# FFN transposes moved from TensorE to VectorE squares and a trip through DRAM, `down` two blocks behind, weights issued by GpSimd

## The reference, cut to what matters

```python
logits = jnp.einsum('btd,de->bte', x, gate_w)
probs = jax.nn.softmax(logits, axis=-1)
expert_weights, expert_indices = jax.lax.top_k(probs, TOP_K)
...
for i in range(E):
    wi = jnp.where(expert_indices == i, expert_weights, 0.0).sum(-1)
    h = jax.nn.silu(jnp.einsum('btd,df->btf', x, w1[i])) * jnp.einsum('btd,df->btf', x, w3[i])
    out = out + jnp.einsum('btf,fd->btd', h, w2[i]) * wi[..., None]
```

## Time and profile before

| | |
|---|---|
| median of 3 runs | 488.11 us (488.01 to 489.12) |
| the profiled execution: its own time | 488.38 us |
| its span, first to last instruction | 486.7 us |
| TensorE matmuls busy | 422.2 us (87% of the span) |
| VectorE busy | 257.6 us (53%) |
| ScalarE busy | 192.5 us (40%) |
| GpSimd busy | 157.4 us (32%) |
| moved by DMA | 50.92 MB |
| mean granted clock of TensorE | 0.935 of full |

### The profile page before, as it was taken

How to read it: one execution, slowest core, us unless ns; L and a number is a source line. 1 busy time by engine, 2 the same in 40 slices (tenths; PEclk the granted TensorE clock), 3 DMA queues, 4 the chain that set the end, 5 groups by cost and what they waited for, 6 DMA issues and landing times.

```text
span 486.7 us, 10406 instructions
## 1 busy us (share of the span) xinstructions
PE 422.2 (87%) x2557; PEld 367.1 (75%) x2558; DVE 257.6 (53%) x673; ACT 192.5 (40%) x334; POOL 157.4 (32%) x130
## 2 busy tenths in 40 slices
PE   0668985237999999999999999999999999999980
PEld 0556874225788888888889888888888898888870
DVE  7877867988454356433553653365355334652230
ACT  3446445113343354334544453444455224542220
POOL 5454440022033224222532342243235222432321
PEclk9979795558899999999999999999999999999996
DMA  6856788300718111911137118112811211111120
GB/s 196 303 179 211 262 267 248 132 23 22 272 24 282 31 32 22 291 32 22 22 71 252 22 27 285 32 22 46 277 22 22 32 32 22 24 30 32 22 32 11
DMA packets 33076, 50.92 MB, mean 105 GB/s; under 512 B 3335, under 2 KB 25095, under 8 KB 33063
## 3 DMA queue, kind: packets, MB, share of 16 engines
q1 hardware_dynamic: 24983, 38.44, 23.7%
q0 software_dynamic: 8080, 12.33, 13.0%
HBM read 39.36 MB, written 11.40 MB: 104 GB/s over the span
## 4 chain that ended last, share of the span: by engine, by line
PE 75%; DVE 5%; issue 2%; DMA 2%; POOL 1%; ACT 0%; DVEq 0%; POOLq 0%; ACTq 0%
PE bank L1319 65%; PE bank L1342 6%; PE bank L1326 2%; PE bank L1252 1%; DMA dg<-depool_rows,plugi 1%; DMA out<-yblk,itok 1%; PE bank L1273 1%; POOL dg L441 1%; DVE split L1117 0%; DVE split L321 0%; DVE batch L985 0%; PE bank L1198 0%; POOL out L480 0%; DVE onehot_lo L981 0%; DVE st L818 0%
## 5 line engine op out<-in xcount | busy, mean ns | idle before, releaser
L1319 PE MATMUL bank<-split,xT_hi 128*128 x592 | 167.9, 406 | 5.4 <-DVEq L1136 4.1
L1091 DVE TENSOR_TENSOR hmul<-gact,bank 128x512 f32<-128x512 f32 x74 | 50.9, 688 | 148.5 <-ACT gact L609 148.5
L1319 PEld LDWEIGHTS bank<-split,xT_hi 128*128 128x128 f32 x592 | 107.7, 192 | 27.0 <-issue 6.1
L480 POOL DMA_INDIRECT out<-yblk,itok x37 | 79.2, 2140 | 150.9 <-ACT yblk L616 143.4
L1319 PE MATMUL bank<-split,hT 128*128 (+1 forms) x888 | 115.2, 286 | 1.0 <-DVE hT L1097 0.7
L1319 PEld LDWEIGHTS bank<-split,hT 128*128 128x128 f32 x888 | 108.5, 191 | 1.4 <-DVE hT L1097 0.9
L609 ACT ACTIVATE gact<-bank 128x512 f32<-128x512 f32 x74 | 44.2, 598 | 164.3 <-PE bank L1319 153.4
L1319 PE MATMUL bank<-split,xT_lo 128*128 x296 | 94.2, 399 | 0.0
L472 POOL DMA_INDIRECT xblk<-z_rows,gidx x40 | 40.7, 1018 | 108.4 <-DVE gidx L1104 102.5
L321 DVE TENSOR_TENSOR split<-raw,split (+1 forms) x22 | 50.4, 2292 | 37.1 <-ACT split L315 35.9
L1319 PEld LDWEIGHTS bank<-split,xT_lo 128*128 128x128 f32 x296 | 56.2, 190 | 13.6
(11 more groups left out here) (182 smaller groups left out, 309.8 us busy)
## 6 DMA issues: line engine op xcount, KB each, us to landing
raw<-in_L_ffn_w SPq DMA_DIRECT2D x24, 1024.0 KB
ctx_sb<-in_ctx SPq DMA_DIRECT2D x4, 1024.0 KB, 6.4
x_all<-in_x SPq DMA_DIRECT2D x4, 512.0 KB, 8.3
depool_rows<-gact SPq DMA_DIRECT2D x4, 512.0 KB, 3.0
out<-x_all SPq DMA_DIRECT2D x4, 512.0 KB
z_rows<-z SPq DMA_DIRECT2D x4, 512.0 KB, 3.4
xblk<-z_rows,gidx POOLq DMA_INDIRECT x40
out<-yblk,itok POOLq DMA_INDIRECT x37
```

Source lines behind the costliest of these rows:

```text
L480: pool.indirect_dma_start(out[:, :], bass.IndirectOffsetOnAxis(ap=itok[:, q:q + 1], axis=0), yblk[:, q, :], None, compute_op=ALU.add).then ...
L1091: dve.tensor_tensor(hmul[:, cols], gact[:, cols], p_lin[part][:, :], ALU.mult)\
L1319: mm = pe.matmul(out_, xp, w_, start=start and n == 0, stop=stop and n == 2)
```

## The change

- `hT` leaves TensorE for all blocks but the last. VectorE transposes `hmul` in squares of 32 x 32 into `swap_in` (`turn`, one instruction for each half). SP writes `swap_in` (512 KB) to `swap_dram`, waits until it has landed, and reads it back into `swap_out` in another order (`exchange`), which moves the squares to their places. ScalarE makes `hT_hi` from `swap_out` by one instruction of 128 x 1024, and VectorE `hT_lo`.
- `down`, `y`, `meta` and `add_rows` are two blocks behind, not one. Blocks 0 and 1 stand outside of the loop; TABLE has one more column, `blocks_i` holds the count less two, and `drain` transposes the last block on TensorE and then does two `down`.
- ScalarE's `y` stands ahead of the weight split in a step, not behind it.
- `raw_load` of experts 1 to 7 goes from SP to GpSimd.
- For the first expert `lo_ready` is raised by 2 ahead of its w2 part and by 1 behind it; before, by 3 behind it. The list of weights and that split come behind both halves of `h` in the first step.
- The rows of zeros at the end of `out` are written by three transfers, not two.

```diff
-TABLE = 1 + 2 * STEP_PAIRS + 3
+TABLE = 2 + 2 * STEP_PAIRS + 3
+Q = 32
+NQ = P // Q
...
+        swap_dram = nc.dram_tensor("swap_rows", (2, P, F), f32, kind="Internal").ap()
+        swap_in = sb("swap_in", [P, 2, NQ, KF, Q], f32)
+        swap_out = sb("swap_out", [P, 2, NQ, KF, Q], f32)
...
-            body(0, 0, 0, step_word(eng, 0))
+            for i in range(2):
+                body(i, i, 0, step_word(eng, i))
             with eng.Fori(0, STEP_PAIRS) as pair:
-                word = step_word(eng, pair * 2 + 1)
+                word = step_word(eng, pair * 2 + 2)
                 with eng.If(word & F_RUN):
-                    body(pair * 2 + 1, 1, pair, word)
-                    word = step_word(eng, pair * 2 + 2)
+                    body(pair * 2 + 2, 0, pair + 1, word)
+                    word = step_word(eng, pair * 2 + 3)
                     with eng.If(word & F_RUN):
-                        body(pair * 2 + 2, 0, pair + 1, word)
-
-        def block_count(eng):
+                        body(pair * 2 + 3, 1, pair + 1, word)
...
-                for e, m in parts[max(k - 1, 0):k] if k < B + 1 else parts[k - 1:]:
-                    raw_load(sp, e, e, s["raw_ready"] if e else s["raw_first"], (m,))
-
-
-            sp.wait_ge(s["lo_first"], 3)
-            sp.wait_ge(s["raw_ready"], RAW_SEM)
-            sp.wait_ge(s["xT_done"], 1)
-            raw_load(sp, 2, 0, s["raw_ready"])
+                for e, m in parts[max(k - 1, 0):k]:
+                    raw_load(sp, e, e, s["raw_first"], (m,))
+
+
             sp.wait_ge(s["table_ready"], 1)
 
+            def exchange(i, q, half):
+
+                sp.wait_ge(s["swap_ready"], 2 * (i + 1))
+                if after(i, 2):
+                    settle(sp)
+                    sp.wait_ge(s["hTlo_ready"], i - 1)
+                sp.dma_start(swap_dram[q], swap_in[:, q].rearrange("p b k t -> p (b k t)")).then_inc(parked[q], 16)
+                sp.wait_ge(parked[q], 16 * (half + 1))
+                sp.dma_start(swap_out[:, q].rearrange("p a k t -> p a (k t)"),
+                             swap_dram[q].rearrange("(a j) (b c) -> (j b) a c", a=NQ, b=NQ)).then_inc(swapped[q], 16)
+
             def step(i, q, half, word):
-                with sp.If(word & F_LOAD):
-                    e = expert(word).with_bounds(min_val=0, max_val=E - 4)
-                    sp.wait_ge(s["lo_ready"], e * 3 + 6)
-                    settle(sp)
-                    sp.wait_ge(s["raw_ready"], RAW_SEM * (e + 2))
-                    settle(sp)
-                    raw_load(sp, e + 3, (e + 1) & 1, s["raw_ready"])
-
+                exchange(i, q, half)
+
+            less_two = blocks_less_two(sp)
             over_steps(sp, step)
...
+            raw_load(pool, 1, 1, s["raw_ready"])
...
-            def step(i, q):
+            def step(i, q, half, word):
 
                 pool.wait_ge(s["xT_done"], i + 2)
                 block_rows(i + 3, 1 - q)
-                if not isinstance(i, int):
-                    add_rows(i - 1, 1 - q)
-
-            step(0, 0)
-            with pool.Fori(0, STEP_PAIRS) as pair:
-                with pool.If(step_word(pool, pair * 2 + 1) & F_RUN):
-                    step(pair * 2 + 1, 1)
-                    with pool.If(step_word(pool, pair * 2 + 2) & F_RUN):
-                        step(pair * 2 + 2, 0)
-            at_end(pool, blocks, add_rows)
-            pool.wait_ge(s["added_rows"], OUT_INIT + blocks * 16)
+                if after(i, 2):
+                    add_rows(i - 2, q)
+                if not after(i, 1):
+                    pool.wait_ge(s["lo_first"], 3)
+                    pool.wait_ge(s["raw_ready"], RAW_SEM)
+                    settle(pool)
+                    raw_load(pool, 2, 0, s["raw_ready"])
+                with pool.If(word & F_LOAD):
+                    e = expert(word).with_bounds(min_val=0, max_val=E - 4)
+                    pool.wait_ge(s["lo_ready"], e * 3 + 6)
+                    settle(pool)
+                    pool.wait_ge(s["raw_ready"], RAW_SEM * (e + 2))
+                    settle(pool)
+                    raw_load(pool, e + 3, (e + 1) & 1, s["raw_ready"])
+
+            def drain(i, q):
+                add_rows(i - 1, 1 - q)
+                add_rows(i, q)
+
+            over_steps(pool, step)
+            at_end(pool, less_two, drain)
...
             def hT(i, q, half):
-                act.wait_ge(s[f"th{half}_done"], i + 1)
-                act.activation(hT_hi[:, q, half * KF // 2:(half + 1) * KF // 2], p_hT[half][:, :], ACT.Copy)\
-                   .then_inc(s[f"hT{half}hi_ready"], 1)
+
+                act.wait_ge(swapped[q], 16 * half)
+                act.activation(hT_hi[:, q].rearrange("p k (a t) -> p a k t", a=NQ), swap_out[:, q], ACT.Copy)\
+                   .then_inc(s["hThi_ready"], 1)
+
+            def hT_last(i, q, part):
+
+                act.wait_ge(s[f"th{part}_done"], 1)
+                ks = slice(part * KF // 2, (part + 1) * KF // 2)
+                act.activation(hT_hi[:, q, ks], p_hT[part][:, :], ACT.Copy)\
+                   .then_inc(s["drainhi_ready"], 1)
...
-                later = not isinstance(i, int) or i > 0
                 silu(i, 0)
-                if later:
-                    hT(i - 1, 1 - q, 1)
                 xT(i + 1, 1 - q)
                 silu(i, 1)
-                hT(i, q, 0)
+                if after(i, 1):
+                    hT(i - 1, 1 - q, half + q)
+                if after(i, 2):
+                    y(i - 2, q)
+                if not after(i, 1):
+                    act.wait_ge(s["list_mm"], 2)
 
                 with act.If(word & F_CHUNK):
                     e = expert(word)
...
                     with act.If(word & F_W2):
                         with act.If(word & F_W3):
                             split_hi(act, raw3, 1)
-                        if later:
+                        if after(i, 1):
                             act.wait_ge(s["y_done"], i)
                         split_hi(act, raw3, 2)
-                if later:
-                    y(i - 1, 1 - q)
 
             def drain(i, q):
-                hT(i, q, 1)
+
+                hT_last(i, q, 0)
+                hT_last(i, q, 1)
+                y(i - 1, 1 - q)
                 y(i, q)
...
                 dve.tensor_tensor(hmul[:, cols], gact[:, cols], p_lin[part][:, :], ALU.mult)\
                    .then_inc(s[f"h{part}_done"], 1)
 
-            def hT(i, q, part):
+            def turn(i, q, half, part):
+
+                dve.wait_ge(s[f"h{part}_done"], i + 1)
+                if after(i, 2):
+                    dve.wait_ge(parked[q], 16 * half)
                 ks = slice(part * KF // 2, (part + 1) * KF // 2)
-                dve.wait_ge(s[f"hT{part}hi_ready"], i + 1)
+                dve.transpose(swap_in[:, q, :, ks, :].rearrange("p b k t -> p k b t"),
+                              hmul[:, part * HALF:(part + 1) * HALF].rearrange("p (k t b) -> p k b t", b=NQ, t=Q))\
+                   .then_inc(s["swap_ready"], 1)
+
+            def hT(i, q):
+
+                dve.wait_ge(s["hThi_ready"], i + 1)
+                dve.tensor_tensor(hT_lo[:, q].rearrange("p k (a t) -> p a k t", a=NQ), swap_out[:, q],
+                                  hT_hi[:, q].bitcast(f32).rearrange("p k (a t) -> p a k t", a=NQ), ALU.subtract)\
+                   .then_inc(s["hTlo_ready"], 1)
+
+            def hT_last(i, q, part):
+
+                dve.wait_ge(s["drainhi_ready"], part + 1)
+                ks = slice(part * KF // 2, (part + 1) * KF // 2)
                 dve.tensor_tensor(hT_lo[:, q, ks].rearrange("p k t -> p (k t)"), p_hT[part][:, :],
                                   hT_hi[:, q, ks].bitcast(f32).rearrange("p k t -> p (k t)"), ALU.subtract)\
-                   .then_inc(s[f"hT{part}lo_ready"], 1)
+                   .then_inc(s["drainlo_ready"], 1)
...
-                later = not isinstance(i, int) or i > 0
+                if not after(i, 1):
+                    dve.wait_ge(s["lo_first"], 2)
+                    dve.sem_inc(s["lo_ready"], 2)
                 h(i, 0)
-                if later:
-                    hT(i - 1, 1 - q, 1)
-                    meta(i - 1, 1 - q)
                 xT(i + 1, 1 - q)
+                turn(i, q, half, 0)
                 next_index(i + 3, 1 - q, half + q + 1)
-                if not later:
+                h(i, 1)
+                turn(i, q, half, 1)
+                if not after(i, 1):
                     weights_out()
-                h(i, 1)
-                hT(i, q, 0)
-                if not later:
                     split_lo(dve, 0, 0, 2, "lo_first")
                     dve.wait_ge(s["lo_first"], 3)
-                    dve.sem_inc(s["lo_ready"], 3)
+                    dve.sem_inc(s["lo_ready"], 1)
+                if after(i, 1):
+                    hT(i - 1, 1 - q)
+                if after(i, 2):
+                    meta(i - 2, q)
...
-            def down(i, q, e, slot, by_halves=False):
-
```

(91 more changed lines are left out.)

20 lines of the change are left out of this document (11 added, 9 removed).

## The result

The changed kernel takes 515.07 us (median, 514.46 to 518.34) against 488.11: 1.056 of the time before, 95% interval 1.053 to 1.059. It is 27 us slower, where 33.6 us faster was forecast. The profiled execution spans 516.7 us; it is the longest of the five runs (518.34 us by its own time), so sums read from its trace are some 3 us above what the median holds.

A forecast was written before the change was run, and what follows sets the result against it. TensorE, busy 87% of the span, was taken as the bound. Gains of 40.4 us less 3.0 (tail), 0.6 (TABLE) and 3.0 (load stalls) gave -33.8 against 488.38: forecast 454.5 us, range 449 to 474.

The forecast's parts named there:

- The loop at 8.68 us: TensorE's block step in the loop falls from 9.56 to 8.68 us as transposes leave; 32.1 us gone in all.
- the sum without load stalls: Whole kernel's forecast time with no stalls from weight loads: 451.5 us, used for the low end of the range.
- Block 1: At the start, `up` of block 1 comes 4.3 us sooner; full clock gives 1.8 more, new `xT_lo` wait costs 0.7.
- TABLE: Longer list operations and rows of odd length from 43 columns for 42 cost 0.6 us, bounds 0 and 1.5.
- Squares: VectorE's two transposes per block take 0.69 us each, bounds 0.4 and 1.4.
- y of block i-2 now stands ahead of the split: Split starts 0.6 us into the next step; VectorE's split, `h`, `xT_lo` end by 6.5, wanted at 8.68: hidden.
- VectorE's order: Sign of a wrong forecast: TensorE's idle time in the loop names `xT_lo`.
- The round trip: Swap to DRAM and back takes 7.6 us, 10.8 beside a load, mean 8.3; hidden up to 9.4, so costed at nothing.
- Gathers behind the weights: x's gathers queue behind GpSimd's weight loads: 3.0 us forecast for six loads; as a rival 458 to 476 us, chance 0.12.
- The lock of GpSimd by VectorE: Rival: each of three load issues loses 0.95 us to VectorE, 3.4 us stall per load; 472 us, chance 0.05.
- Slower than before: the same loop past its point: Rival: mean round trip over 11.4 us makes the loop step over 9.70; at 12.5 it is 510 us; chance 0.09.
- The tail: After the last step's `down`, three adds come close together and the last goes at about 9.4 us: 3.0 us lost.

The follow-up runs named there:

- experiment 3: Changed kernel with VectorE's `meta` first in its step and the weight loads of experts 2 to 7 cut to 3 x 128 KB: 452.71 us, ratio 0.927.
- experiment 1: Changed kernel with VectorE's `meta` of block i-2 moved first in its step, not behind `hT`: 483.46 us, ratio 0.989.
- 6: Changed kernel with ScalarE's `y` put back behind the weight split and `meta` left where the change has it: 483.29 us, ratio 0.989.
- experiment 2: Changed kernel with the weight loads of experts 2 to 7 cut to 3 x 128 KB, most weights left out: 478.51 us, ratio 0.980.
- experiment 4: Kernel before the change, with only the weights of experts 1 to 7 issued by GpSimd: 483.81 us, ratio 0.993.
- experiment 7: Changed kernel with `meta` first on VectorE and the weights issued by SP behind the exchange of the step: 499.03 us, ratio 1.023.

## Why the prediction was wrong

- *The loop at 8.68 us:* right. It is the step in 11 of 35 here and in 34 of 35 of experiment 3. That its 452.71 us lie beside the sum without load stalls (451.5) is in part luck: the start lost 3.4 us more than reckoned and the tail 3 (both below), and behind the last add 4.8 us went away (11.6 to 6.8) that the sum does not have.
- *Block 1:* right for its own wait. From the x transposes of step 0 to those of step 1 are 7.8 us, where it was 14.4. Of the 6.6 us gained 0.9 are transposes that the sum counts elsewhere; 5.7 are left against 4.3 + 1.8. The new wait for the next `xT_lo` was mis-sized: for 0.7 the next step lost 3.1 us in the changed kernel (a wait of 2.9) and 4.1 in experiment 3 (a wait of 2.5, and the half of `up` behind it at a granted clock of 0.66).
- *TABLE:* 0.6 us forecast. The first x transposes start 0.1 to 0.8 us later in the kernels with it (106.28 to 106.98 for 106.22); how much of this is its doing is not shown.
- *Squares:* mis-sized, 1.105 us against 0.69, inside of the bounds. It makes the ring 0.8 us longer; without it the ring would be 9.7, still over 8.68.
- *"y of block i-2 now stands ahead of the split, so the split starts 0.6 us into the next step ... They are wanted at 8.68: hidden."* **This is the step that failed.** I let y wait for `down` only. It also waits for `meta`, which the change puts behind `hT_lo` on VectorE; I counted `meta` among "copies 0.5". So I listed each engine's load, 7.2 us of 8.68, and one in-order chain (from the trip's landing), and missed the ring that needs no trip. Opening it gave 31.6 us in experiment 1, and by 6 either of its sides can be opened. The largest wait of TensorE, for `xT_lo`, is the sign that the prediction gave for "VectorE's order".
- *The round trip:* right where nothing runs beside it (6.9 us for 7.6), mis-sized beside a load. I took half of the bandwidth, as one 128 KB gather suggested, and 10.8 us; it was 12.7 (7.56 and 5.10), with up to 11.3 for one read. But the mean was right: 8.45 us over the 37 trips against my 8.3, and under the 9.4 that I said the in-order engines bear. So it is the averaging that failed. Behind each load after the first, one trip took 12.7 to 13.5 us and the next 8.2 to 8.9, and short trips later did not pay back the stall of TensorE. I had the trip at nothing and 3.0 us for the gathers; the loads cost 36.6 us by experiment 2.
- *Gathers behind the weights:* as a cause of its own it falls (experiment 4). In the changed kernel TensorE waits 8.7 us for them in 6 waits, of which one of 1.1 us, ahead of the first block, is in the kernel before too. So at most 7.6 of the 36.6 us are late gathers beside the exchange; no run removes them alone.
- *The lock of GpSimd by VectorE*, not borne out. The issues of a load take 0.83 us each on the mean, 2.5 for three where I took 5, and moving them to SP made the kernel slower. All 37 adds take 1.55 to 1.68 us: none of them runs beside a split or `hT_lo` here, while beside a split they took 2.5 to 2.9 in the kernel before. The Trainium skill's "SBUF — State Buffer", section "Who interferes with whom", says that a DMA issued from GpSimd can starve of descriptors; no run here shows it.
- *"Slower than before: the same loop past its point"* was the right sign, and its 510 us lie near 515 by luck. Its condition, a mean R over 11.4, was not met (8.45); single trips passed that point beside the loads, and the ring, which it does not have, carried the time the rest of the way.
- *The tail:* 3.0 us of loss forecast. With the end of the last `down` in a step at 0 (492.92 + 2.87 = 495.8) the last add goes at 12.6 us, not at 9.4. The chain of the changed kernel, its last adds:

```profile
498.23 4.80 DMA out<-yblk,itok
...
503.86 3.78 DMA out<-yblk,itok
...
508.42 1.55 POOL out L498
```

Of the 3.2 us more, 0.9 stand ahead of the first add, 1.5 in its landing (4.80 us for the 3.35 of the earlier trace rows), 0.4 in the second's, and 0.4 between landings and issues. In the changed kernel y waited for `meta` again, but this was not what cost the 0.9: with `meta` first, in experiment 3, y is on time, the first add is still issued 2.4 us behind `down`, and the last one goes at 12.5.

## What to carry to other kernels

When work moves between in-order engines, write down for every instruction all that it waits for, small copies as well, and look for a cycle that goes from one engine to the other and back within a step; its length is a lower bound of the step, however idle the engines are. Here one line moved was worth 32 us. A mean is no test for a transfer on such a path: the mean trip was inside its room, and the bursts still cost 37 us. A transfer put on a loop's path must be priced beside the largest burst in the program, and cutting the burst in parts (12 us) and moving it to an idle time (9 us) cost no bytes.

## What the runs showed of the hardware

- A transpose in squares of 128x512 f32 on VectorE takes 1.10 us where an elementwise instruction of the same size takes 0.69.
- A 512 KB write to DRAM takes 3.1 us by itself (experiment 3) and 7.56 beside a load of 3 MB from another queue (changed kernel, at 270.41); the read that follows takes 3.8, and 5.1 and once 11.3 there.
- An indirect add of 128 rows by GpSimd takes 1.59 us and beside VectorE's split, with two inputs in SBUF, 2.5 to 2.9 (the 20 such adds of the kernel before).
- From the issue of the last add to the end of the span are 11.6 us in the two kernels in which SP issues the weights in its loop (475.04 to 486.7, and 483.47 to 495.1 in experiment 7), and 8.1 to 8.3 us where GpSimd does (seven kernels with full loads; 6.8 and 7.0 in the two with small ones). That is most of what experiment 4 gained. What takes these 3.3 us no view shows.
